# Layer norm, 16-head attention and an eight-expert layer on one core: the experts moved one attention step later, the small preparation pieces, routing and scatters laid out anew, and four extra matmuls before the first scores

## What is computed

```python
x = L0_attn_x                              # (4, 1024, 128)
xn = _layernorm(x, axis=-1)
# attention: 16 heads of 8, rotary tables, softmax over 1024 keys
q, k, v = heads(xn @ Wq.T), heads(xn @ Wk.T), heads(xn @ Wv.T)
q = q * cos + rotate_half(q) * sin         # k likewise
attn = softmax(einsum('bhnd,bhmd->bhnm', q, k) * D ** -0.5) @ v
# experts: 8 of them, the two likeliest of each token
g = softmax(xn @ gate_w + gate_b); vals, idx = top_k(g, 2)
h = gelu(xn @ w1 + b1); h = gelu(h @ w2 + b2); y = h @ w3 + b3
out = x + attn + sum(vals * y[idx])
```

## Time and profile before

| | |
|---|---|
| time, median of 3 runs | 672.18 us (671.33 to 673.16) |
| profiled execution | 672.06 us, span of instructions 670.4 us |
| busy | PE 607.3 us (91%), ACT 565.0 us (84%), DVE 243.2 us (36%), POOL 222.0 us (33%) |
| granted TensorE clock, mean | 0.992 of full speed |
| chain that ended last | PE 57%, ACT 19%, issue 13%, DVE 6% |
| first exponential of steps 0, 1, 2, 3, 8, 9 | 24.49, 59.73, 93.25, 127.35, 283.58, 452.71 us |

### The profile page before, as it was taken

One profiled execution on the slowest core, in us unless ns is written; L12 is line 12 of the kernel. 1 busy time (PEld: TensorE's weight loads), 2 busy tenths in 40 slices (PEclk: granted clock), 3 DMA queues, 4 the chain that ended last, 5 costly groups with the idle time before them and its releaser, 6 DMA issues.

```text
span 670.4 us, 12951 instructions
## 1 busy us (share of the span) xinstructions
PE 607.3 (91%) x4234; PEld 264.4 (39%) x4234; DVE 243.2 (36%) x699; ACT 565.0 (84%) x696; POOL 222.0 (33%) x235
## 2 busy tenths in 40 slices
PE   9689999999999999888999999997888888888885
PEld 5223433323222232223888888881222222222221
DVE  5573346652332333113555555540302022121213
ACT  3689898899999999998555555559999999999995
POOL 2501023417666866530122221224232332333300
PEclk9799999999999999999999999998999999999999
DMA  7793014324333334495334343311212111122204
GB/s 216 198 388 105 18 47 142 111 81 140 126 119 127 118 119 145 128 299 126 64 75 82 66 82 71 76 50 51 67 40 71 54 51 51 55 62 63 67 5 130
DMA packets 84054, 68.50 MB, mean 102 GB/s; under 512 B 47281, under 2 KB 61137, under 8 KB 84017
## 3 DMA queue, kind: packets, MB, share of 16 engines
q1 hardware_dynamic: 77328, 53.78, 27.5%
q0 software_dynamic: 5968, 13.51, 6.7%
q10 hardware_dynamic: 720, 0.71, 0.4%
HBM read 33.51 MB, written 33.42 MB: 100 GB/s over the span
## 4 chain that ended last, share of the span: by engine, by line
PE 57%; ACT 19%; issue 13%; DVE 6%; DMA 1%; POOL 1%; ACTq 1%; DVEq 0%; SPq 0%; POOLq 0%
PE ps L1139 20%; ACT probs L540 19%; PE ps L1162 10%; PE ps L1124 8%; PE ps L1172 5%; PE ps L1155 5%; PE ps L1092 4%; PE ps L1148 3%; PE ps L1057 1%; DVE o_sb L738 1%; DVE xn_all L631 1%; DVE stats L594 1%; DMA q_st<-parts 1%; ACTq L536 1%; DMA x_all<-in_L_attn_x_dram 1%
## 5 line engine op out<-in xcount | busy, mean ns | idle before, releaser
L540 ACT ACTIVATE probs<-ps 128x1024 f32<-128x1024 f32 x512 | 481.6, 1041 | 20.1 <-PE ps L1124 13.3
L1139 PE MATMUL ps<-probs,v_st 128*32 128x512 f32 x2048 | 275.3, 609 | 44.9 <-ACT probs L540 33.7
L1124 PEld LDWEIGHTS ps<-q_st,k_st 32*128 32x128 f32 x1024 | 49.5, 182 | 225.2 <-ACT probs L540 192.1
L1124 PE MATMUL ps<-q_st,k_st 32*128 32x512 f32 x1024 | 130.4, 498 | 8.3 <-DMA q_st<-parts 3.8
L555 ACT ACTIVATE work<-ps,work 128x256 f32<-128x256 f32 x156 | 70.7, 474 | 65.6 <-PE ps L1162 65.2
L477 POOL DMA_INDIRECT work<-slots_y_d,slot_i x64 | 60.5, 945 | 122.3 <-PE ps L1139 110.5
L1139 PEld LDWEIGHTS ps<-probs,v_st 128*32 128x32 f32 x2048 | 41.0, 108 | 119.2 <-ACT probs L540 91.4
L437 POOL DMA_INDIRECT slots_x_d<-xn_all,slot_i x64 | 62.1, 971 | 46.7 <-PE ps L1139 32.1
L738 DVE COPY o_sb<-ps 128x512 f32<-128x512 f32 x32 | 22.1, 691 | 151.8 <-PE ps L1139 151.8
L1162 PE MATMUL ps<-work 128*128 128x256 f32 x312 | 73.9, 380 | 0.1
L460 POOL DMA_DIRECT2D slots_y_d<-work x39 | 27.9, 714 | 129.3 <-DVE work L886 124.8
(11 more groups left out here) (142 smaller groups left out, 351.0 us busy)
## 6 DMA issues: line engine op xcount, KB each, us to landing
k_d<-parts SPq DMA_DIRECT2D x8, 1024.0 KB, 5.6
q_d<-parts SPq DMA_DIRECT2D x8, 1024.0 KB, 4.9
q_st<-q_d SPq DMA_DIRECT2D x30, 256.0 KB, 2.9
k_st<-k_d SPq DMA_DIRECT2D x30, 256.0 KB, 2.9
slots_x_d<-parts SPq DMA_DIRECT2D x5, 1024.0 KB, 11.7
work<-slots_x_d SPq DMA_DIRECT2D x80, 64.0 KB, 2.3
slots_y_d<-work POOLq DMA_DIRECT2D x39, 128.0 KB, 2.2
parts<-in_L_ffn_w_dram SPq DMA_DIRECT2D x16, 128.0 KB
```

The lines of the kernel that those rows point to most:

```text
L540: nc.scalar.activation(probs[:, j % PROB_RING, 2 * pair:2 * pair + 2, :], score_slot(j, pair).rearrange("p (h n) -> p h n", h=2), ACT.Exp, ...
L1124: ins = nc.tensor.matmul(score_slot(j, h // 2)[:, (h % 2) * HALF:(h % 2 + 1) * HALF], k_st[32 * h:32 * h + ROWS, mt * P:(mt + 1) * P], q_s ...
L1139: ins = nc.tensor.matmul(o_ps[32 * h:32 * h + 32, :], v_st[:, mt, h, :], probs[:, j % PROB_RING, h, :], start=(mt == 0), stop=(mt == MT - 1))
```

## The change

`SPLIT` goes from 9 to 10 and `GATHER` from 5 to 6. `prepare_batches` becomes `prepare_rows(b)`: at block (0, 0) the statistics and inverses of all 24 tiles, but the normalisation of batch 1 alone; batch 2 follows at (0, 13), batch 3 at (1, 3). The values of batches 1 to 3 are made two row tiles at a time (four jobs a batch, not three). The four norms of batch 0 move from (0, 13), (0, 14), (1, 11), (1, 12) to (0, 3), (0, 4), (0, 6), (0, 7). From block 10 to 47 every block without a turn has a job: rows and values of batch 1, then the projections of batch 1 alternating with the rows and values of batches 2 and 3. The 44 projection pieces and norms that are left are spread evenly over blocks 52 to 132. Routing runs in blocks 45 and 49 to 69, `count` at block 58. The scatters begin at block 70, keep off the two blocks behind each second swap part, and end with tile 31 at block 153, which is (9, 9). The zero fill moves to blocks 2 to 6 of step 1. Four matmuls of 128x512 on zeros (`WARM_AGAIN`) stand before PE's first scores.

```diff
-SPLIT = 9
-GATHER = 5
+SPLIT = 10
+GATHER = 6
+WARM_AGAIN = 4
+def value_tiles(b, n):
+    return range(3 * n, min(3 * n + 3, BT)) if b == 0 else range(2 * n, 2 * n + 2)
 def plan_jobs():
...
+    fixed = {0: ("values", 0, 2), 3: ("norm", 0), 4: ("norm", 1), 6: ("norm", 2), 7: ("norm", 3), 58: ("count",),
+             BLOCKS * 8 + 12: ("bound",)}
+    first = rows(1) + vals(1)
+    others = rows(2) + vals(2) + rows(3) + vals(3)
+    p = pieces(1)
+    while p or others:
+        first += p[:1] + others[:1]
+        p, others = p[1:], others[1:]
+    places = [n for n in range(10, 50) if n not in turns and n not in fixed]
+    fixed.update(zip(places, first))
...
+    places = [n for n in range(last + 5, BLOCKS * 8 + 6) if n not in turns and n not in fixed]
+    step = len(places) / len(todo)
+    fixed.update((places[int(step * i)], job) for i, job in enumerate(todo))
...
+for _n, _block in enumerate([45] + [n for n in range(49, 80) if n % MT and n != 58][:18]):
+    ROUTE[divmod(_block, BLOCKS)] = _n
+def plan_scatter():
+    routed = max(t * BLOCKS + j for t, j in ROUTE) + 1
+    swaps = [t * BLOCKS + j for (t, j), job in JOBS.items() if job[0] == "swap" and job[2]]
+    starts, n = {}, routed
+    while len(starts) < TILES:
+        if not any(s <= n < s + 2 for s in swaps):
+            starts[n] = len(starts)
+            n += 1 + (len(starts) % 3 == 0)
+        n += 1
+    return starts
...
-            for r in range(SLOT_ROOM // 8):
-                sp.dma_start(slots_x_d[...], parts[:, :, 3, :]...)
...
+                    if t == 1 and 2 <= j < 2 + SLOT_ROOM // 8:
+                        r = j - 2
+                        sp.wait_ge(S["scores_done"], t * UNITS + 2 * j)
+                        sp.dma_start(slots_x_d[...], parts[:, :, 3, :]...)
...
-            starts = {3 * BLOCKS + MT + 5 * i // 2: i for i in range(TILES)}
+            starts = plan_scatter()
...
-            with act.Fori(0, 2) as t:
+            with act.Fori(0, 3) as t:
                 attention_exps(t)
             act.wait_ge(S["max_made"], 1)
...
-            def prepare_batches():
-                statistics(BT, TILES)
-                invert_rest()
-                for b in range(1, B):
-                    for k in range(BT):
-                        ins = normalise_row_tile(b * BT + k)
-                    ins.then_inc(S["batch_rows_made"], 1)
+            def prepare_rows(b):
+                if b == 1:
+                    statistics(BT, TILES)
+                    invert_rest()
+                for k in range(BT):
+                    ins = normalise_row_tile(b * BT + k)
+                ins.then_inc(S["batch_rows_made"], 1)
...
                             load_v(0, 1, True)
-                            prepare_batches()
+                            prepare_rows(1)
...
+                    if (t, j) in ((0, 13), (1, 3)):
+                        prepare_rows(2 + t)
...
+            for _ in range(WARM_AGAIN):
+                nc.tensor.matmul(bank(0), zeros[:, 0:P], xnT[:, 0, 0:HALF], start=True, stop=True)
             pe.wait_ge(S["proj_read"], 4)
             scores(0, 0, first=True)
```

More of the change, by code:

```diff
@@ L61, in plan_jobs, with pieces @@
-    early = [(1, j) for j in (13, 14, 15)] + [(2, j) for j in (0, 2, 3, 4, 5, 6, 7, 8, 10, 11, 13, 14, 15)] + [(3, j) for j in (0, 2, 3, 4)]
-    later = [(3, j) for j in (6, 8, 11, 13, 14)] + [(t, j) for t in (4, 5, 6) for j in (0, 2, 3, 5, 6, 8, 10, 11, 13, 14)]\
-        + [(7, j) for j in (0, 2, 3, 5, 6)]
-    for b in range(1, B):
[L65 to L72, removed]
+    def pieces(b):
+        return [(kind, 4 * b + k, part) for k in range(4) for kind in ("plain", "swap") for part in range(2)]
@@ new lines, in rows, with vals @@
+    def rows(b):
+        return [("rows", b, half) for half in range(2)]
+    def vals(b):
+        return [("values", b, n) for n in range(BT // 2)]
+    turns = {BLOCKS * t + MT + 1 for t in range(SPLIT)} | {BLOCKS * t + 1 for t in range(1, SPLIT)}
+    fixed = {0: ("values", 0, 2), 3: ("norm", 0), 4: ("norm", 1), 6: ("norm", 2), 7: ("norm", 3), 58: ("count",),
[3 more added lines that the diff above has]
+    p = pieces(1)
@@ new lines, in plan_jobs @@
+    while p or others:
+        first += p[:1] + others[:1]
+        p, others = p[1:], others[1:]
+    places = [n for n in range(10, 50) if n not in turns and n not in fixed]
+    assert len(first) <= len(places), (len(first), len(places))
+    fixed.update(zip(places, first))
+    last = max(n for n, job in fixed.items() if job[0] == "swap")
+    todo = [("norm", 4 + k) for k in range(4)]
+    for b in (2, 3):
+        for n, job in enumerate(pieces(b)):
+            todo.append(job)
+            if n % 4 == 3 and n > 3:
+                todo.append(("norm", 4 * b + n // 4 - 1))
+        todo.append(("norm", 4 * b + 3))
@@ L73, in plan_jobs @@
+    places = [n for n in range(last + 5, BLOCKS * 8 + 6) if n not in turns and n not in fixed]
+    step = len(places) / len(todo)
+    fixed.update((places[int(step * i)], job) for i, job in enumerate(todo))
+    jobs = {divmod(n, BLOCKS): job for n, job in fixed.items()}
     for t in range(SPLIT):
@@ L439, in scatter @@
                         in_=xn_all[:, i, :], in_offset=None).then_inc(S["x_scattered"], 16)
-            starts = {3 * BLOCKS + MT + 5 * i // 2: i for i in range(TILES)}
+            starts = plan_scatter()
+            assert max(starts) <= (SPLIT - 1) * BLOCKS + MT + 2
             for t in range(SPLIT):
@@ L547, in _ @@
             nc.scalar.activation(rt[:, 1], rt[:, 0], ACT.Exp).then_inc(S["exp_made"], 1)
-            with act.Fori(2, SPLIT) as t:
+            with act.Fori(3, SPLIT) as t:
                 attention_exps(t)
@@ L762, in route @@
                 if n == 0:
-                    dve.wait_ge(S["aux_read"], AUX[("values", B - 1, 2)] + 1)
+                    dve.wait_ge(S["aux_read"], AUX[("values", B - 1, BT // 2 - 1)] + 1)
                     link(nc.vector.tensor_reduce(rs[:, 0], logits[:], AX.X, ALU.max))
@@ L1054, in project_values @@
             def project_values(b, n, dst):
-                for k in range(3 * n, min(3 * n + 3, BT)):
-                    ins = nc.tensor.matmul(dst[:, (k - 3 * n) * VG:(k - 3 * n + 1) * VG], xnT[:, b, k * P:(k + 1) * P], wvg[:],
+                for i, k in enumerate(value_tiles(b, n)):
+                    ins = nc.tensor.matmul(dst[:, i * VG:(i + 1) * VG], xnT[:, b, k * P:(k + 1) * P], wvg[:],
                                            start=True, stop=True)
```

18 lines of the change are left out of this document (8 added, 10 removed).

## The result

The changed kernel takes 686.14 us (685.89 to 686.79, 4 runs), the kernel before 671.75 us beside it (671.18 to 673.16, 4 runs); the ratio is 1.0211 (95% interval 1.0192 to 1.0229). The forecast was 682 us in a range of 674 to 688, slower with a chance of 0.82. The profiled execution took 686.18 us, its span 684.4 us.

A forecast was written before the change was run, and what follows sets the result against it. ACT's exponentials set the pace, with time lost where PE jobs or waits stop them; the expert part is PE-bound. The terms -1.9 + 6.2 - 1.9 + 1.9 - 0.6 - 0.7 + 3.0 + 1.7 + 2.5 = +10.2 on 672.06 gave 682 us, range 674 to 688.

The forecast's parts named there:

- dummies: Before PE's first scores: four dummy matmuls keep the clock up and save ACT's standstill, -1.9 us.
- wait at the second norm, with its clock loss: Step 0: norm (0, 4) waits for DVE to read norm (0, 3), +6.2 us; the gap halves PE's clock, +1.9.
- old wait for `rows` gone: Step 0: the second `rows` job no longer waits for DVE's normalisation of batches 2 and 3, -1.9 us.
- pieces, routing: Values two tiles at a time over three batches, -0.6 us; routing portions delaying fewer copies in steps 2 and 3, -0.7.
- handover, with its clock loss: Last step to experts: the later last scatter delays SP's row and weight loads, +3.0 us; half rate after PE's gap, +1.7.
- six tiles in a step: Steps behind the experts: the sixth gathers land late, `combine` delays the copy of the sums, 0.5 in five steps, +2.5 us.
- all three waits: Main case: waits at the second norm, the expert handover and the late combine all occur; 678 to 687 us, chance 0.62.
- signs that the forecast named: Profile: ACT idle some 6 us, norm waiting, clock 1.0 at 24-31 us, PE gap 2-4 before `layer1`, copies 0.2-0.9 late.
- a fixed 42.0: Step 0: the time in us when ACT starts block 6, against 35.8 undisturbed, giving +6.2.
- the expectation of e4: Theory written for e4: the dummies keep the clock up and save 1.9 us, so without them about 688 us.
- loads without company in the queue: Expert handover: row loads no longer sharing the queue with another expert's could win back up to 1.3 of 3.8 us.
- The rival that paid off (DVE in time): Step 0: DVE reads the first norm by 33.8, no wait or clock loss, 667 us; chance of faster 0.12.

The follow-up runs named there:

- e4: The changed kernel without the four dummy matmuls (WARM_AGAIN = 0): 685.32 us, ratio 1.0187 to the kernel before.
- e5: The kernel before with the four dummy matmuls as its only change: 683.44 us beside 683.11, ratio 1.0005.
- e1: The changed kernel with DVE's first preparation piece cut up, batch 1 normalised in block (0, 8): 677.92 us, ratio 1.008 to the kernel before.
- e2: The changed kernel with the last expert's weights loaded at block 9, ahead of the wait for the scatters: 678.39 us, ratio 1.0077.
- e3: The changed kernel with a step's gathers started every 2.5 blocks instead of every 3: 680.48 us, ratio 1.0108.
- e12: The changed kernel itself, run once more on another chip: 692.29 us beside 684.2 for the kernel before, ratio 1.0122.
- e11: e9 with routing portions and count kept out of blocks right before a copy, scatters spaced once in five: 672.32 us, ratio 0.9829.
- e6: The kernel before with SPLIT = 10 and GATHER = 6 and nothing else: 692.9 us beside 683.11, ratio 1.0135.
- the 668 above: Worked out, not run: the changed kernel with all three repairs, without standstills, some 668 us where the kernel before takes 672.
- e9: Changed kernel with preparation cut up, weights ahead of the scatters' wait, gathers every 2.5 blocks: 673.46 us beside 684.2, ratio 0.9835.
- e7: The same kernel as e9, run in another group: 675.46 us beside 683.11 for the kernel before, ratio 0.9882.
- e10: The kernel of e8 run a second time: 711.11 us beside 684.2 for the kernel before, ratio 1.0377.
- e8: The changed kernel with denser scatters, the last starting in block 127 instead of 153: 711.93 us, ratio 1.0412 to the kernel before.
- the first group: The runs e1 to e4, timed on one chip beside the kernel before, which took 673.06 us there.

## Why the prediction was right, step by step

| step of the forecast | forecast | measured |
|---|---|---|
| dummies | -1.9 | -0.9 in the first three blocks (-2.1 in four other traces), not told from 0 by the times of e4 and e5 |
| wait at the second norm, with its clock loss | +6.2 +1.9 | +7.4 (block 5: 9.23 for 1.81; e1 takes 7.4 back) |
| old wait for `rows` gone | -1.9 | -1.8 (block 9: 1.97 for 3.81) |
| pieces, routing | -0.6 -0.7 | -1.0 over steps 1 to 8, -0.4 in other blocks of step 0 |
| handover, with its clock loss | +3.0 +1.7 | +4.1 +2.5 (e2 takes 6.7 back) |
| six tiles in a step | +2.5 | +2.4 (e3 takes it back) |
| start | 0 | +1.6, not of the change |

The mechanisms stood: all three waits are where they were forecast, with the work queued behind them that was named, and each goes when its cause alone is taken away. Of the signs that the forecast named, one failed: the clock didn't stay up behind the first scores. Three sizes were off, and they don't cancel: the sum was +10.2, the measured difference of the profiled runs 14.0.

**The dummies.** The term -1.9 assumed that the one gap of 3.8 us costs the clock. The clock fell at 28.6 after smaller gaps, with the dummies in place; the kernel before had shown as much at 454.5, where the longest gap of PE was 1.25 us. The sum itself had both sides of the other effect, that DVE sets when block 6 begins: its +6.2 is the wait up to a fixed 42.0, and had the dummies been forecast to save less, the wait would have been shorter by as much. Only the expectation of e4 took the 1.9 as a gain of the whole. Dummies, wait and clock together were +6.2 and measured +6.5. The Trainium skill ("TensorE: Matmul & The Clock Gate", the table of why this matters for kernels) warns of idle gaps between bursts; the trace agrees for the two long gaps here, 5.85 and 4.07 us, but not for the stretch at 28.6, where the longest gap was 1.28.

**The handover.** I took 3.0 because loads without company in the queue might win back 1.3. They won nothing: eight row loads took SP 5.13 us (4.92 before), and from there to DVE's first copy it was 10.5 (10.1). The landing itself was quicker than the 2.6 that I took from the gathers: 2.24 us. The estimate of 2.2 from the page "DMA: Bandwidth & Descriptors" of the Trainium skill (anatomy of one DMA) agrees with this scatter; the median of the 64 is 2.6, and the slowest lands after 5.35. The clock took 2.5 rather than 1.7, since the half rate lasted 6.8 us, not 3.4. That too is a matter of the run: in e1, e3 and e12, with the same handover, it lasted 3.4 us and took 1.2 to 1.3, and the stretch was 5.0, 5.4 and 5.3 us longer than before instead of 6.7. In e4 it was 7.7 longer.

**Smaller sizes.** The portions in front of a copy and `count` cost the changed kernel 2.3 us (blocks 57, 59 and 65 take 3.26, 2.50 and 2.26 us; 1.98, 1.82 and 1.97 in e11), where I had taken 1.9. In the term for six tiles the rows give 0 to 0.6 us of lateness, not the 0.2 to 0.9 written (511.3 plus 3.4 is 514.7, the start of the copy before); that 0.5 a step came out is partly luck.

**The start.** The profiled execution of the changed kernel meets a half-rate stretch at 11.5 us, before anything that differs. The first exponential comes at 24.4 to 24.9 in nine traces and at 25.9 to 26.2 in five (the changed kernel, e1, e2, e5, e6); the changed kernel itself has it at 26.12 in one and at 24.44 in the other (e12). Of the 14 us these 1.6 belong to the run.

The rival that paid off (DVE in time) wasn't what happened, but e1 shows what it would have been worth: with DVE's piece cut up, the new layout's step 0 is 3.0 us shorter than before, and steps 1 to 8 are 1.0 shorter than before in the changed kernel. By the same sum as for the 668 above, the change's own idea was worth some 4 us; three waits cost 16.5. Which part of those 4 us comes from the pieces of values, the routing, the zero fill or the spacing of the scatters wasn't run piece by piece.

What stays open: why identical code shows 2.51 us in block 57 in some traces (e9, e12) and 3.26 in others (the changed kernel, e7, e10), what stops all engines behind rows of indirect DMAs, and what decides in which stretches the clock falls.

## What to carry to other kernels

- When a job goes to an earlier place on one engine, ask where its reader stands in its own engine's order. PE had room for the norm at block 3; DVE was booked until what would have been block 8, and PE's next job waits for the reader.
- A wait in a DMA queue delays everything behind it. Moving one load of weights in front of the wait was worth 5.0 to 6.7 us, without touching what the wait is for.
- When a producer gets one more item per round, look at when the last item lands against the deadline of the next thing in the consumer's order, not at the consumer's busy share (36% here).

## What the runs showed of the hardware that I hadn't expected

- In the two groups where the kernel before took 683 to 684 us instead of 672, ACT stood for 2.4 to 3.4 us at the end of twelve of the eighteen rows of six or eight scatter DMAs in e5, e6, e8 and e10, and for 1.2 to 2.0 us at the others. For 2.1 us of one such stop in e5 and 1.7 of one in e8 no engine started an instruction. Behind rows of four to six gathers it mostly stood for 1.3 to 1.7 us. Spacing the scatters decided by 25 us (steps 4 to 8 take 179.7 us in e8 and 154.9 in e12). In the traces of the kernel before, the changed kernel and the first group, rows of six leave ACT running in steps 4 to 8.
- Filling a gap of PE kept the clock up only in some traces, and what it won was lost again at the next wait for DVE (e12 against the first trace of the same kernel, 1.2 us either way).
- The clock fell to 1.2 GHz in the middle of work with no idle time of PE above 1.3 us near it (28.6 us in the changed kernel, 28.75 in e5), and in the prologue in five of the fourteen traces.
